# A two-layer cross-attention kernel: a quarter of the layer 1 masks moves from TensorE to GpSimd, and the barrier between the layers goes

## The reference

```python
# layer 1, mask_BxSxS2_if1 is (16, 256, 1601)
scores = jnp.einsum('bhqd,bhkd->bhqk', q, k) / jnp.sqrt(jnp.float32(DK))
scores = jnp.where(mask[:, None, :, :] == 0, NEG, scores)      # NEG = -65504
attn = jax.nn.softmax(scores, axis=-1)
out = jnp.einsum('bhqk,bhkd->bhqd', attn, v)
```

## Time and profile before

| | us |
|---|---|
| median of 3 runs | 5445.89 (5444.5 to 5447.28) |
| profiled execution | 5421.1 |
| its span | 5419.8 |
| PE busy | 4887.3 (90%) |
| DVE busy | 3598.6 (66%) |
| ACT busy | 2794.9 (52%) |
| POOL busy | 641.3 (12%) |

### The profile page before, as it was taken

One profiled execution on the slowest core, in us unless ns is written; L12 is line 12 of the kernel. 1 busy time (PEld: TensorE's weight loads), 2 busy tenths in 40 slices (PEclk: granted clock), 3 DMA queues, 4 the chain that ended last, 5 costly groups with the idle time before them and its releaser, 6 DMA issues.

```text
span 5419.8 us, 103495 instructions
## 1 busy us (share of the span) xinstructions
PE 4887.3 (90%) x41312; PEld 2745.4 (51%) x41312; DVE 3598.6 (66%) x8383; ACT 2794.9 (52%) x5505; POOL 641.3 (12%) x660
## 2 busy tenths in 40 slices
PE   5888888888888888889899999999999999999999
PEld 2455555555555555554455544554455444554456
DVE  4666666666666666566667777777777777777774
ACT  1565565656555556665454444444445444444454
POOL 1111111110111111011110101101010101001000
PEclk7799898989999999897899999999999999999999
DMA  2112222222212222222222222222222222222222
GB/s 60 34 45 52 44 46 52 58 54 50 53 45 43 48 58 54 58 49 70 59 72 69 77 65 70 76 69 65 70 72 69 75 61 78 74 70 64 73 49 65
DMA packets 167992, 327.09 MB, mean 60 GB/s; under 512 B 25656, under 2 KB 76624, under 8 KB 167520
## 3 DMA queue, kind: packets, MB, share of 16 engines
q1 hardware_dynamic: 167520, 320.49, 24.3%
HBM read 237.40 MB, written 4.19 MB: 45 GB/s over the span
## 4 chain that ended last, share of the span: by engine, by line
PE 39%; DVE 8%; SPq 2%; POOL 1%; issue 1%; DMA 1%; ACT 1%; DVEq 0%
PE sums L695 7%; PE a L658 7%; PE d L771 6%; PE a L759 5%; PE a L666 4%; DVE d L811 3%; SPq L1072 2%; PE d L679 1%; PE d L601 1%; PE d L581 1%; PE d L733 1%; PE a L608 1%; PE a L641 1%; DMA kc<-k_hi 1%; PE d L614 1%
## 5 line engine op out<-in xcount | busy, mean ns | idle before, releaser
L967 ACT ACTIVATE probs_c<-a 128x512 f32<-128x512 f32 (+1 forms) x3584 | 1833.9, 563 | 1994.5 <-PE a L666 1992.7
L811 DVE CUSTOM_DVE_ANT_0 d<-d,mcross_q 128x404 f32<-128x404 f32 x2048 | 1138.0, 606 | 341.6 <-PE d L679 337.6
L803 DVE TENSOR_REDUCE chunk_max<-d 128x2 f32<-128x808 f32 x1024 | 1003.2, 998 | 289.0 <-PE d L679 280.5
L695 PE MATMUL sums<-probs_c,vc 128*32 128x256 f32 x13312 | 1119.9, 410 | 13.4 <-PEq L1234 13.2
L666 PE MATMUL a<-qc,kc 25*128 25x256 f32 (+1 forms) x6656 | 931.1, 341 | 129.7 <-ACT probs_c L967 98.5
L666 PEld LDWEIGHTS a<-qc,kc 25*128 25x128 f32 (+1 forms) x6656 | 543.0, 187 | 825.9 <-issue 393.3
L679 PE MATMUL d<-kc,qc 24*128 24x404 f32 x4096 | 912.4, 458 | 47.0 <-DVE chunk_max L811 12.9
L771 PE MATMUL d<-w_back,hidden 128*128 128x128 f32 x4352 | 558.4, 283 | 28.8 <-DVE chunk_max L811 28.8
L759 PE MATMUL a<-xT_e,w_in 128*128 128x256 f32 x2176 | 576.5, 412 | 0.0
L771 PEld LDWEIGHTS d<-w_back,hidden 128*128 128x128 f32 x4352 | 533.5, 197 | 66.8 <-DVE chunk_max L811 39.5
L658 PE MATMUL a<-mcross_k,ident_b 128*128 128x512 bf16 (+1 forms) x1792 | 547.4, 379 | 12.4 <-ACT probs_c L967 12.2
(11 more groups left out here) (157 smaller groups left out, 4441.6 us busy)
## 6 DMA issues: line engine op xcount, KB each, us to landing
w_in<-in_experts SPq DMA_DIRECT2D x272, 256.0 KB, 3.1
w_back<-in_experts SPq DMA_DIRECT2D x272, 256.0 KB, 2.9
kc<-k_hi SPq DMA_DIRECT2D x1024, 50.0 KB
ctxT<-in_ctxT SPq DMA_DIRECT2D x32, 800.5 KB, 5.2
kc<-k_lo SPq DMA_DIRECT2D x512, 50.0 KB
mask_words<-in_mcross SPq DMA_DIRECT2D x32, 800.5 KB
mask_words<-in_mcrossT SPq DMA_DIRECT2D x32, 768.0 KB
out_x<-xe SPq DMA_DIRECT2D x32, 128.0 KB, 1.8
```

The lines of the kernel that those rows point to most:

```text
L695: last = pe.matmul(acc[HP * j:HP * j + HP, :], T["vc"][x.p][0:x.kn, v0:v0 + HP], probs_of(T, x)[0:x.kn, j, half:half + S], start=x.j == 0, ...
L803: done = dve.tensor_reduce(T["chunk_max"][:, x.g % 2, x.i, x.j:x.j + 2, x.c], tile[:].rearrange("p (h n) -> p h n", h=2)[:, :, 0:CHUNK], A ...
L811: done = dve.tensor_tensor_reduce(some, some, mask, 1.0, -3e38, ALU.add, ALU.max, T["chunk_max"][:, x.g % 2, x.i, x.j + h, x.c:x.c + 1])
L967: act.activation(probs_of(T, x)[0:x.kn, x.j, 0:n], tile[0:x.kn, 0:n], ACT.Exp, scale=SCALE).then_inc(M["a_read"], 1)
```

## The change

Layer 1 scores of head j = 0 of each group no longer begin with a mask on PE (`masked(x)` is true from `BY_POOL` = 1 on). POOL instead works on that head's exponentials after ACT: it cuts them off at 2.0 (`min`), then multiplies them in place with `factors`, which are 1 where a key may be seen and 0 where it may not. The first sum of each key pair waits for the product (`multiplied`).

The factors are made once for each layer 1 sequence, after the last mask part. A new PE step `MF` multiplies a matrix of ones (`ones_b`) with all 13 tiles of `mcross_k`, which counts the masked keys of each query; DVE turns the count into `allowed` (1, or 2 where all keys of a query are masked). Five new DVE steps `MB` write `mcross_k / 2**100 + allowed` into `factors`, three key tiles at a time and the last one alone. `MF` takes a place in ring `d`, and both are woven into the stretch of `cross_masks` with costs 1.5 and 0.8, which moves the mask loads and conversions a little earlier in it.

The causal masks of layer 0 and the self masks of layer 1 now share one pair of tiles (`mask_q`, `mask_k`), which frees memory for the factors. The barrier between the pieces is gone: rounds -1 to 32 are one piece.

```diff
+
+BY_POOL = 1
+
+FACTORS = ((0, 3), (3, 6), (6, 9), (9, 12), (12, 13))
 EXPERT_SLOTS = 2
...
         "EF": 0.87, "ES": 1.8, "OT": 0.9, "OPT": 0.45, "OPM": 0.3, "XT": 0.45, "EBT": 0.3, "EBM": 0.3, "RT": 0.2,
-        "NC": 0.45, "NS": 0.45, "SV": 0.5}
+        "NC": 0.45, "NS": 0.45, "SV": 0.5, "MF": 1.5, "MB": 0.8}
 LATER = {"XT": 1.5, "RM1": 1.5, "LN1": 1.5, "RM2": 3.5, "LN2": 4.0, "OT": 2.0, "OPT": 1.5, "OPM": 1.0, "RT": 3.0,
          "R2": 3.0, "R3": 3.0, "EBT": 1.5, "EBM": 1.0, "NS": 1.5, "ML": 8.0}
-D_RING = ("QP", "SV", "MS", "NS", "MC", "NC", "OT", "OPM", "KC", "VC", "RT", "EBM", "ES")
+D_RING = ("QP", "SV", "MS", "NS", "MC", "NC", "OT", "OPM", "KC", "VC", "RT", "EBM", "ES", "MF")
 A_RING = ("XT", "SS", "WS", "SC", "OPT", "EBT", "EF")
...
             self.at["mcross", p] = out[-1]
+        out.append(self.put(("found", p), "MF", "mask", p=p))
+        for i in range(len(FACTORS)):
+            out.append(self.put(("factors", p), "MB", p=p, i=i))
+            out[-1].of["found"] = self.at["found", p]
         return out
...
                 sc.of["mask"] = self.at.get(("mcross", p))
+                sc.of["factors"] = self.at.get(("factors", p))
+            if j == BY_POOL - 1:
+                self.at["by_pool"] = sc
             steps.append(sc)
                 step.of["sc"] = sc
+                if l and kt % 2 == 0:
+                    step.of["by_pool"] = self.at["by_pool"]
                 if kt == 0:
...
             groups += x.last
+        elif x.kind == "SC" and x.l == 1 and x.j == BY_POOL - 1:
+            x.c = by_pool = by_pool + 1
         elif x.kind == "EF" and x.l == 1:
...
+
+def masked(x):
+
+    return x.l == 1 and x.j >= BY_POOL
...
                         pe.wait_ge(M["masks_made"], nth(y.of["mself"]))
-                mask = (T["mself_q"] if y.l else T["causal_q"])[:].rearrange("p a b -> p (a b)")
+                mask = T["mask_q"][:].rearrange("p a b -> p (a b)")
                 for h in range(2):
...
                     pe.wait_ge(M["masks_made"], nth(y.of["mask"]))
-                if y.l:
+                if masked(y):
                     n = len(key_tiles(y))
...
                                      T["kc"][rows, y.g, kt * P:kt * P + y.kn], T["qc"][y.p][rows, y.g, :],
-                                     start=not y.l, stop=not y.l or ends)
+                                     start=not masked(y), stop=not masked(y) or ends)
                     if ends:
...
                 pe.wait_ge(M["a_read"], in_ring(x.of["sc"]))
+            if "by_pool" in x.of:
+                pe.wait_ge(M["multiplied"], x.of["by_pool"].c)
             acc = T["sums"][:, x.g % 2 * S:(x.g % 2 + 1) * S]
...
                                  start=True, stop=True)
+            last.then_inc(M["d_made"], 1)
+        elif x.kind == "MF":
+            pe.wait_ge(M["masks_made"], nth(x.of["mask"]))
+            for kt, (_, kn) in enumerate(spans(SK, P)):
+                last = pe.matmul(tile[:, 0:S], T["ones_b"][0:kn, :], T["mcross_k"][x.p][0:kn, kt, :], start=kt == 0,
+                                 stop=kt == KT - 1)
             last.then_inc(M["d_made"], 1)
...
             dve.tensor_scalar(dest, view, 0, -BIG, ALU.is_equal, ALU.mult).then_inc(M["masks_made"], 1)
+        elif x.kind == "MF":
+            dve.tensor_scalar(T["allowed"][:], tile[:, 0:S], -BIG * SK, 1.0, ALU.is_equal, ALU.add).then_inc(M["d_read"], 1)
+        elif x.kind == "MB":
+            dve.wait_ge(M["d_read"], in_ring(x.of["found"]))
+            first, last = FACTORS[x.i]
+            rows = slice(0, P if last < KT else SK - first * P)
+            dve.scalar_tensor_tensor(out=T["factors"][x.p][rows, first:last, :], in0=T["mcross_k"][x.p][rows, first:last, :],
+                                     scalar=1.0 / BIG, in1=wide(T["allowed"][rows, :], last - first), op0=ALU.mult,
+                                     op1=ALU.add).then_inc(M["factors_made"], 1)
         elif x.kind in ("RT", "R2", "R3"):
...
                                ALU.subtract).then_inc(M["q_made"], 1)
+        elif x.kind == "SC" and x.l == 1 and x.j == BY_POOL - 1:
+            n = len(key_tiles(x))
+            probs = probs_of(T, x)[0:x.kn, 0:BY_POOL, 0:n * S]
+            factors = T["factors"][x.p][0:x.kn, 2 * x.i:2 * x.i + n, :].rearrange("p a b -> p (a b)")
+            pool.wait_ge(M["a_read"], in_ring(x))
+            pool.tensor_scalar(probs, probs, 2.0, 1.0, ALU.min, ALU.mult).then_inc(M["cut_off"], 1)
+            if "factors" in x.of:
+                pool.wait_ge(M["factors_made"], nth(x.of["factors"]))
+            pool.wait_ge(M["cut_off"], x.c)
+            pool.tensor_tensor(probs, probs, wide(factors, BY_POOL), ALU.mult).then_inc(M["multiplied"], 1)
         elif x.kind == "RS":
...
     dve.wait_ge(set_up, 16 * (len(loads) + 4))
-    dve.tensor_copy(T["causal_q"][:], T["probs_c"][0][:, 0:QT, 0:S])
-    dve.tensor_copy(T["causal_k"][:], T["probs_c"][1][:, 0:QT, 0:S])
+    dve.tensor_copy(T["mask_q"][:], T["probs_c"][0][:, 0:QT, 0:S])
+    dve.tensor_copy(T["mask_k"][:], T["probs_c"][1][:, 0:QT, 0:S])
     dve.tensor_copy(T["ident_b"][:], T["ident"][:])
+    dve.memset(T["ones_b"][:], 1.0)
     for part in range(3):
...
     restart()
-    rounds(-1, B - 1)
-    restart()
-    rounds(B, LAST)
+    rounds(-1, LAST)
```

More of the change, by code:

```diff
@@ L441, in numbered @@
     slots = {"d": 2, "a": 3}
-    moved, loaded, groups, tanhs = {}, {}, 0, 0
+    moved, loaded, groups, tanhs, by_pool = {}, {}, 0, 0, 0
     place = {id(x): i for i, x in enumerate(order)}
@@ L501 @@
          "rt_exp", "rt_second", "rt_gate", "rt_done", "bias_added", "silu_done", "key_high", "rows_inverted",
-         "masks_made", "x_loaded", "ctx_loaded", "words_loaded")
+         "masks_made", "factors_made", "cut_off", "multiplied", "x_loaded", "ctx_loaded", "words_loaded")
 MOVES = HG * 3
@@ L606, in tensor_program @@
                     pe.wait_ge(M["d_read"], in_ring(y.of["ns"]))
-                mask = (T["mself_k"] if y.l else T["causal_k"])[:].rearrange("p a b -> p (a b)")
+                mask = T["mask_k"][:].rearrange("p a b -> p (a b)")
                 pe.matmul(T["a"][y.slot][:], T["ident_b"][:], mask, start=True, stop=False)
@@ L1105, in mask_tile @@
     if x.i < 2:
-        return (T["mself_q"], T["mself_k"])[x.i][:]
+        return (T["mask_q"], T["mask_k"])[x.i][:]
     if x.i < 4:
@@ L1141, in program @@
     T = {
-        "ident": sb("ident", [P, P]), "ident_b": sb("ident_b", [P, P], BF16), "iota": sb("iota", [P, E0]),
-        "causal_q": sb("causal_q", [P, QT, S], BF16), "causal_k": sb("causal_k", [P, QT, S], BF16),
+        "ident": sb("ident", [P, P]), "ident_b": sb("ident_b", [P, P], BF16), "ones_b": sb("ones_b", [P, P], BF16), "iota": sb("iota", [P, E0]),
+        "mask_q": sb("mask_q", [P, QT, S], BF16), "mask_k": sb("mask_k", [P, QT, S], BF16),
         "w_pad": sb("w_pad", [P, 2, 3, NG, P]), "b_pad": sb("b_pad", [P, 2, 3, NG]),
@@ L1153, in program @@
         "q_sum": sb("q_sum", [P, NG, S]), "q_high": sb("q_high", [P, NG, S], F32R),
-        "mself_q": sb("mself_q", [P, QT, S], BF16), "mself_k": sb("mself_k", [P, QT, S], BF16),
         "mcross_q": pair("mcross_q", [P, QT, SK], BF16), "mcross_k": pair("mcross_k", [P, KT, S], BF16),
+        "factors": pair("factors", [P, KT, S], BF16), "allowed": sb("allowed", [P, S], BF16),
         "probs_c": pair("probs_c", [P, HG, BANK]), "probs_s": sb("probs_s", [P, HG, BANK]),
```

## The result

The changed kernel takes 5534.61 us (median, 5530.67 to 5539.43) against 5445.19 us: a ratio of 1.0163, 95% interval 1.0148 to 1.0177, slower by 89 us. Forecast were 5459 us, 5410 to 5505; the time lies above the range. The profiled execution has a span of 5529.4 us at a granted clock of 0.919; before it was 5419.8 us at 0.933.

What follows compares the result with a forecast made beforehand. Layer 1 was taken to be set by PE's stream, with DVE the one engine near enough to matter. Terms -59 + 26 + 5 + 48 + 5 - 18 + 6 = +13 on 5445.9 gave 5459 us, range 5410 to 5505.

Steps and rivals of the forecast that it cites:

- masks off PE: Layer 1 scores: 448 masks fewer on PE save 59 us, bounds 0 to 91.
- MF with its wait, MB and DVE: Layer 1: MF on PE +26, its wait +5, and half of DVE's added 96 us reaching PE, +48.
- POOL late: Layer 1 sums: late product or splits, +5 (0 to 40); as rival, 0.10, PE waits in every tight beat, 5550.
- barrier: Border between the pieces: PE's 13.19 us idle gap and low clock after it go, -18 (-13 to -25).
- clock: Layer 1's granted clock drops slightly with fewer masks on PE: +6 us, at most 36.
- the layer 1 clock stays at 0.96 or 0.97: Sign to look for: layer 1's granted clock, profiled at 0.97, hardly moves.
- clock falls towards layer 0's: Rival, chance 0.08: layer 1's clock falls towards 0.91, costing +36 in place of +6, 5489 us.
- I take the whole 0.22 for the 64% that do not wait: Layer 1 beats: a removed mask saves 0.22 us where the second mask awaits no exponential, nothing elsewhere; -59 together.
- the removal does nothing: Rival, chance 0.07: exponentials set the layer 1 beats, so masks off PE save 15 instead of 59; 5503 us.
- the three lines that the prediction named for 30 to 50 us: Sign: idle PE before L601, L771 and L679 caused by DVE grows by 30 to 50 us.
- line 881's median: Sign: this DVE conversion, 1.377 us in the middle, rises above 1.4 because of newly busy POOL.
- DVE's additions are hidden: Rival, chance 0.32: DVE's 28% idle in layer 1 absorbs its new work, +10 in place of +48; 5421 us.

Runs made afterwards that it cites:

- e2: Changed kernel without MF, MB, POOL's two instructions and PE's wait for them; head 0 of layer 1 unmasked: 5384.3 us, ratio 0.9894.
- e1: Kernel before with its rounds in one piece (no barrier) and nothing else of the change: 5432.4 us, ratio 0.9982.
- e9: Changed kernel without MF and MB, constant factors of 1.0; POOL's cut-off and product and PE's wait kept, head 0 unmasked: 5451.9 us.
- e4: Changed kernel without POOL's cut-off; the product stays: 5475.8 us, ratio 1.0066.
- e6: Changed kernel without MF, MB and cut-off; POOL's product with constant factors of 1.0 and PE's wait kept, head 0 unmasked: 5453.9 us.
- e5: Changed kernel with MF and MB but without POOL's two instructions and PE's wait; head 0 unmasked: 5416.2 us, ratio 0.9946.
- e12: Changed kernel without MF, MB and cut-off; POOL's product on a tile nobody reads, PE not waiting, head 0 unmasked: 5442.7 us.
- e3: Changed kernel with all its additions and the mask products on PE for head 0 kept as well: 5545.6 us, ratio 1.0198.
- e14: Changed kernel with MF and MB; POOL's cut-off and product on a tile nobody reads, constant factor, PE not waiting, head 0 unmasked: 5511.6 us.
- e7: Changed kernel with the cut-off as one operation (minimum alone) instead of two: 5538.6 us, ratio 1.0171.
- e15: e12 with POOL's product on 16 columns in place of 512: 5385.2 us, ratio 0.9903.
- e8: Changed kernel, whole, with MF and MB woven later into the round, 0.66 to 0.95: 5466.9 us, ratio 1.0038.
- e10: Changed kernel without POOL's cut-off and with MF and MB later in the round, 0.66 to 0.95: 5480.2 us, ratio 1.0065.
- e16: e12 with two one-input multiplications on POOL in place of the two-input product: 5422.7 us, ratio 0.9948.
- e17: e2 with an idle product on DVE ahead of the mask steps and gate step that POOL's product lengthens: 5428.1 us.

## Why the prediction was wrong

The forecast's terms, except its sixth, are prices of work, and are compared with span x clock; the clock has a term of its own.

| term | forecast | measured at full clock | from |
|---|---|---|---|
| masks off PE | -59 | -29 | e2 - e1 |
| MF with its wait, MB and DVE | +79 | +57 to +68 | after - e9, e4 - e6, e5 - e2 |
| POOL late | +5 | +3 to +6 | e6, e9, e12 - e2; after - e4 gives -8 |
| barrier | -18 | -6 to -8 | e1 - before |
| sum | +7 | +28 | after - before |
| clock | +6 | +62 | lost, after - before |

With the bias of the split counted, the clock's +62 is some 46 to 52 us of the 89 and the other terms are 37 to 43, where +6 and +7 were forecast.

**The step that failed is the clock.** It was worked out from the masks taken off PE and from idler PE in layer 0, with +36 as its bound. Taking the masks off does not lower it (e2), though with the additions there they hold it up by 30 us (e3). The other parts lower it, through delays that cost little full-clock time: POOL's product by itself +50 to +62 (e12, e6), the cut-off +65 with the real factors beside it at their place and 0 without (e4, e9), PE's wait for the product +24 (e14). The forecast "the layer 1 clock stays at 0.96 or 0.97" failed with it: 0.94. The 0.97 that it started from was also that of an unusually fast execution; e1 has 0.96. The rival "clock falls towards layer 0's", given 0.08, named the right resource for the wrong reason and stopped at 36 us. The second miss is the masks' saving, twice too large (below).

**POOL's price.** The cut-off was read from a multiplication's row; a minimum takes 1.96 us, not 0.70, so the two take 3.12 us and not 1.97. By the rival "POOL late" that should have meant waits at the sum in every tight beat; the real waits are 16 (18 us; under 10 us was forecast), which fits the prediction's remark that the lag mostly is far longer. Nor does the length beyond the product's 1.1 us explain the loss: e7 shortens the cut-off by 0.45 us for nothing, and e9 costs what e6 does. Up to there it does (e15). The price was wrong in its number, and on the path that it was worked out for, the sums, it did little harm.

**The masks.** "I take the whole 0.22 for the 64% that do not wait" was twice too much. In the kernel after, a tight beat with one mask has its scores at 2752.67 and 2754.25:

```profile
2752.67 0.38 PE L687 MATMUL a<-qc,kc 25*128 25x256 f32 x2
...
2753.20 1.08 ACT L1005 ACTIVATE probs_c<-a 128x512 f32<-128x512 f32 x2 [0.17 <-PE a L687]
...
2753.94 0.38 PE L679 MATMUL a<-mcross_k,ident_b 128*128 128x512 bf16 x1 [0.78 <-ACT probs_c L1005]
...
2754.25 0.38 PE L687 MATMUL a<-qc,kc 25*128 25x256 f32 x2
```

1.58 us, where 1.46 was forecast (the prediction's own limit, the mask 1.17 after the scores, gives 1.49) and two masks took 1.54. The mask starts 0.20 us after the first exponential should be done (half of 1.08 from 2753.20), and the handover was put at 0.1. The exponential sets this beat, as the rival "the removal does nothing" had it; of its -15 and my -59, -29 is between. L658's 1792 instructions became 1344, as forecast.

**DVE and MF** were about right at full clock, and so was the mechanism: MB at 0.98, and over all lines where PE waits for chunk_max its wait went from 108 to 142 us. But of the three lines that the prediction named for 30 to 50 us, L601 went from 41.2 to 62.7 and the other two fell, +13 together; the rest is at products that now stand behind a conversion, such as L743 above, and at MF itself (11). But line 881's median did not rise above 1.4: its large conversion takes 1.04 on average in the kernel after, and it is small steps that are held up instead. (The low bound of 2.4 us a sequence was a slip too: 3584 columns at that conversion's rate are 2.2.) Half of the cost or more is the place: later in the round it costs 24 to 30 instead of 57 to 68 (e8 - e9, e10 - e6), and L743's wait falls to 2.0 us in e8. "DVE's additions are hidden" (0.32) is refuted by e5. **The barrier's** gap went as forecast; most of its gain did not stay.

**Left open.** How many low stretches a given delay brings: MF and MB alone bring 38 us fewer lost, with POOL's full work 23 more. L743's wait cannot be it alone, as e5 has it too (16.2 us) and loses least. Nor is it how late DVE is in sum: DVE is busy 3678 us in e4 and 3684 in the kernel after, with other steps held up, and the second loses 65 us more; e10 has more DVE time than e8 (3691 and 3678) and no more gain. Which of DVE's steps count for the clock is not shown. And through what e16 still loses 24 to 35 us (the first against the kernel before on the same chip). POOL work that leaves DVE wholly alone was not tried.

## What to carry to other kernels

Read span and granted clock of several executions first, and price work by their product and the clock apart; an edit whose product hardly moves can still cost a per cent through the clock. Work given to an idle engine is not free because it is short of the bound: here 1.1 us of POOL per 6 us cost more than the masks' whole gain (58 to 70 us against 48), in good part, as far as e16 and e17 show it, by holding up small steps of DVE. Before a wait is put down to the change, look for the same wait in the kernel before, and in the experiment without the suspected work: q_sum's wait for POOL was as long where POOL had nothing new to do. Take a price from a row of the same operation, not of the same instruction kind.

## What the runs showed of the hardware

A minimum of 128x512 on POOL takes 1.5 us alone and 1.96 with a multiplication behind it in the same instruction, three times the two multiplications of the same size (0.63 to 0.65). One of DVE's steps of two columns takes 0.17 us, 0.50 under POOL's product (another such step) and 1.0 under its full work. And a DVE that is late by 22 to 33 us in all, spread over 2780, went with 35 to 62 us more lost to TensorE's clock (e17, e12, e6, e9), while MF and MB alone went with 38 less (e5).
